# Row maxima from 48-row products in the array's row halves, with stacks loaded for two groups at a time, in a cross-attention and ternary-FFN kernel

## What is computed

```
q = layernorm(x) @ Wq ; k, v = split(ctx @ Wkv)      # 32 heads of 16
q, k = axial_rope(q, pos), axial_rope(k, pos)
w = softmax(q k^T / 4)                               # 4 x 32 heads, 512 x 512 each
x = x + (w v) @ Wout + bout
h = gelu(bitlinear(layernorm(x), w_fc))              # ternary weights, quantised activations
x = x + bitlinear(h, w_proj)
```

## Time and profile before

| | |
|---|---|
| Median of 3 runs | 771.08 us (770.41 to 771.29) |
| Profiled execution | 771.07 us, span in the trace 769.3 us |
| TensorE busy | 754.0 us (98%) |
| VectorE busy | 661.9 us (86%) |
| ScalarE busy | 481.9 us (63%) |
| GpSimd busy | 430.1 us (56%) |
| Chain that ended last | TensorE 87% of the span |
| DMA | 117.24 MB, mean 152 GB/s |
| Granted TensorE clock | 1.00 over nearly all of the span |

### The profile page before, as it was taken

How to read it: one execution, slowest core, us unless ns; L and a number is a source line. 1 busy time by engine, 2 the same in 40 slices (tenths; PEclk the granted TensorE clock), 3 DMA queues, 4 the chain that set the end, 5 groups by cost and what they waited for, 6 DMA issues and landing times.

```text
span 769.3 us, 11882 instructions
## 1 busy us (share of the span) xinstructions
PE 754.0 (98%) x3886; PEld 342.9 (45%) x3886; DVE 661.9 (86%) x927; ACT 481.9 (63%) x830; POOL 430.1 (56%) x501
## 2 busy tenths in 40 slices
PE   5999999999999999999999999999999999999998
PEld 3887877333323322332233223345554455555443
DVE  7888999788888888889888888479998889998895
ACT  4787766787788777788878888765323433333330
POOL 5787776675345446456446557665564845564310
PEclk9999999999999999999999999999999999999999
DMA  8588996555587778887777896326566575544655
GB/s 279 176 219 249 267 260 167 138 141 132 139 170 147 152 157 138 161 179 144 151 162 162 180 192 154 73 69 136 116 135 124 101 147 114 119 96 96 114 106 136
DMA packets 178862, 117.24 MB, mean 152 GB/s; under 512 B 119746, under 2 KB 150514, under 8 KB 178802
## 3 DMA queue, kind: packets, MB, share of 16 engines
q1 hardware_dynamic: 178802, 116.49, 67.6%
HBM read 64.50 MB, written 25.43 MB: 117 GB/s over the span
## 4 chain that ended last, share of the span: by engine, by line
PE 87%; DMA 4%; DVE 2%; ACT 2%; POOL 2%; SPq 1%; issue 1%; POOLq 0%; DVEq 0%; ACTq 0%
PE banks L741 15%; PE banks L725 14%; PE banks L1040 14%; PE banks L1025 14%; PE banks L702 12%; PE banks L297 8%; PE banks L1006 6%; DMA stack_words<-max_rows 2%; PE banks L328 1%; DMA max_rows<-max_parts 1%; PE banks L713 1%; SPq L619 1%; PE banks L280 1%; SPq L257 1%; POOL attn_words L527 0%
## 5 line engine op out<-in xcount | busy, mean ns | idle before, releaser
L815 ACT ACTIVATE probs_words<-banks 128x512 f32<-128x512 f32 x512 | 290.7, 596 | 70.7 <-PE banks L725 57.9
L795 DVE TENSOR_REDUCE maxima<-banks 128x2 f32<-128x1024 f32 x240 | 283.2, 1216 | 41.4 <-PE banks L702 41.4
L725 PE MATMUL banks<-stack_words 98*128 98x512 bf16 x512 | 173.6, 382 | 2.2 <-DMA stack_words<-max_rows 1.2
L702 PE MATMUL banks<-stack_words 96*128 96x512 bf16 x480 | 143.0, 379 | 0.0
L741 PE MATMUL banks<-probs_words,late_words 128*32 128x512 f32 x1024 | 136.4, 605 | 0.0
L725 PEld LDWEIGHTS banks<-stack_words 98*128 98x128 bf16 x512 | 48.7, 96 | 158.0 <-ACT probs_words L815 109.1
L1025 PE MATMUL banks<-ternary_words,late_words 128*128 128x512 f16 x512 | 113.1, 379 | 0.0
L1040 PE MATMUL banks<-ternary_words,stack_words 128*128 128x512 f16 x512 | 112.9, 379 | 0.0
L1224 ACT ACTIVATE probs_words<-probs_words,h_moments 128x2048 f32<-128x2048 f32 (+1 forms) x17 | 32.2, 1901 | 120.6 <-DVE h_moments L1103 120.6
L826 POOL TENSOR_SCALAR neg_max<-maxima 128x16 f32<-128x16 f32 x32 | 8.3, 260 | 145.4 <-DVE maxima L795 145.4
L1025 PEld LDWEIGHTS banks<-ternary_words,late_words 128*128 128x128 f16 x512 | 49.8, 98 | 60.5 <-issue 0.8
(11 more groups left out here) (157 smaller groups left out, 1065.2 us busy)
## 6 DMA issues: line engine op xcount, KB each, us to landing
o_rows<-late_words SPq DMA_DIRECT2D x32, 256.0 KB, 3.4
k_parts<-ternary_words SPq DMA_DIRECT2D x48, 128.0 KB, 3.0
q_parts<-ternary_words SPq DMA_DIRECT2D x48, 128.0 KB, 2.5
stack_words<-q_parts SPq DMA_DIRECT2D x32, 192.0 KB, 3.2
stack_words<-k_parts SPq DMA_DIRECT2D x96, 64.0 KB, 2.7
stack_words<-k_parts SPq DMA_DIRECT2D x32, 192.0 KB, 2.7
attn_words<-in_x_dram SPq DMA_DIRECT2D x16, 256.0 KB, 4.0
probs_words<-in_L_ffn_w_fc_dram SPq DMA_DIRECT2D x16, 256.0 KB, 3.6
```

Source lines behind the costliest of these rows:

```text
L702: mm = self.nc.tensor.matmul(self.score_slot[j % 2][:, i], self.mem.q_stack[0:STACK, slot, head, c * P:(c + 1) * P], self.mem.k_stack[0:ST ...
L725: self.nc.tensor.matmul(self.st_bank[(g * 16 + k) % self.ST_BANKS], self.mem.k_stack[0:STACK + 2, slot, head, c * P:(c + 1) * P], self.mem ...
L795: dve.tensor_reduce(self.maxima[:, g % 2, 2 * j:2 * j + 2], self.score_slot[j % 2], AX.X, ALU.max).then_inc(self.scores_read, 1)
L815: act.activation(self.probs[:, c, head, :], self.st_bank[(g * 16 + k) % self.ST_BANKS], ACT.Exp, scale=1 / math.sqrt(HEAD)).then_inc(self. ...
```

## The change

`scores` and `early_scores` use three of the six part products (48 rows, `MAIN`) in place of six (96). The stacks are laid out so that for heads 0 and 1 the three lie on partitions 0 to 47, for heads 2 and 3 on 64 to 111. A place of `scores` now does head h and head h + 2 of the same chunk: two 48-row products, one on each half of the array's rows, one to each bank of the slot. The turned products run over 114 rows, of which 16 are zero: rows 96 to 111 for the first two heads, 0 to 15 for the others. The zeros come from a strip that GpSimd clears (`row_zeros`, after its third `spread`) and two DMAs (`clear_rows`, SP step 4); begin_late_stacks copies them for a third pair of slots, in `late_words`.

Stacks are loaded for two groups at a time, in two halves of 7 and 8 DMAs with 2 KB rows; a group's first product waits for all 15. Pair 0 is loaded whole at the projection's step 8, pair 1 at steps 12 and 14; in the attention a half follows per step. The scores run two places ahead (`LEAD`). `save_sums` moves behind the third reduction of a step.

```diff
-STACK = 6 * HEAD
+MAIN = 3 * HEAD
+HALF_ROWS = 64
+MAX_ROW = HALF_ROWS + MAIN
+STACK = MAX_ROW + 2
...
-STACK_LOADS = DMA * 7
+STACK_PAIRS = 3
+STACK_LOADS = DMA * (7 + 8)
...
+    def clear_rows(self, sp, rows_set):
+
+        sp.wait_ge(self.row_ones_set, 2)
+        for first, heads in ((STACK - 2 - HEAD, slice(0, 2)), (0, slice(2, 4))):
+            sp.dma_start(self.mem.both_stacks[first:first + HEAD, :, heads].rearrange("p n h c -> p n (h c)").bitcast(F32),
+                         self.row_zeros.unsqueeze(1).to_broadcast([HEAD, 2 * STACK_SLOTS, SEQ])).then_inc(rows_set, DMA)
...
+    def load_stacks(self, sp, pair, half):
+
+        mem, g = self.mem, 2 * pair
+        for i in range(2):
+            sp.wait_ge(self.prj.parts_stored[i], PAIR_STORES * (g // HG + 1))
+        need(sp, self.st_ready, (g - 2 * STACK_PAIRS + 2) * 16)
+        for t, where, runs in ((0, mem.q_parts, self.Q_RUNS[half]), (1, mem.k_parts, self.K_RUNS[half])):
+            src = where[g:g + 2].rearrange("g t (d h) c -> (t d) g (h c)", h=GH)
             for to, part, count in runs:
...
+    def wait_stacks(self, pe, g):
+        pe.wait_ge(self.stacks_loaded[g // 2 % STACK_PAIRS], (g // 2 // STACK_PAIRS + 1) * STACK_LOADS)
+
+    def main_product(self, out, g, head, c):
+
+        first = head // 2 * HALF_ROWS
+        rows = slice(first, first + MAIN)
+        return self.nc.tensor.matmul(out, self.stack(0, g)[rows, head, c * P:(c + 1) * P], self.stack(1, g)[rows, head, :],
+                                     start=True, stop=True)
...
-        for i in range(2):
-            c = j % 2 * 2 + i
-            mm = self.nc.tensor.matmul(self.score_slot[j % 2][:, i],
-                                       self.mem.q_stack[0:STACK, slot, head, c * P:(c + 1) * P],
-                                       self.mem.k_stack[0:STACK, slot, head, :], start=True, stop=True)
+        for half in range(2):
+            mm = self.main_product(self.score_slot[j % 2][:, half], g, j // CHUNKS + 2 * half, j % CHUNKS)
         mm.then_inc(self.scores_ready, 1)
...
-                              self.mem.k_stack[0:STACK + 2, slot, head, c * P:(c + 1) * P],
-                              self.mem.q_stack[0:STACK + 2, slot, head, :], start=True, stop=True
+                              self.stack(1, g)[0:STACK, head, c * P:(c + 1) * P],
+                              self.stack(0, g)[0:STACK, head, :], start=True, stop=True
...
-            if s < GROUPS and not begun:
-                self.scores(pe, s, 2 * c)
+            if not begun:
+                self.scores_ahead(pe, ahead)
...
+        EARLY_LOADS = {8: (0, (0, 1)), 12: (1, (0,)), 14: (1, (1,))}
...
-                    if j == 1 and s >= 3:
+                    if j == 3 and s >= 3:
                         att.save_sums(dve, s - 3)
...
             pool.wait_ge(att.rows_set, DMA)
+            pool.wait_ge(prj.piece_ready[1], 4)
+            pool.memset(prj.row_zeros, 0.0).then_inc(prj.row_ones_set, 1)
```

More of the change, by code:

```diff
@@ new lines, in stack, with begin_late_stacks @@
+    def stack(self, t, g):
+        return self.stack_pair(t, g // 2)[:, g % 2]
+    def begin_late_stacks(self, sp):
+        late = self.late_stacks.rearrange("p t s h c -> p (t s) h c")
+        for first, heads in ((MAX_ROW - HEAD, slice(0, 2)), (0, slice(2, 4))):
+            rows = slice(first, first + HEAD)
+            sp.dma_start(late[rows, :, heads].rearrange("p n h c -> p n (h c)"),
+                         self.mem.k_stack[rows, :, heads].rearrange("p n h c -> p n (h c)")).then_inc(self.rows_set, DMA)
+        rows = slice(MAX_ROW, MAX_ROW + 2)
+        sp.dma_start(self.late_stacks[rows, 1].rearrange("p s h c -> p (s h) c"),
+                     self.mem.k_stack[rows, 0:2].rearrange("p s h c -> p (s h) c")).then_inc(self.rows_set, DMA)
@@ L778, in tensor_step @@
                 self.scores_turned(pe, turned, 4 * c + 3)
-            if s < GROUPS and not begun:
-                self.scores(pe, s, 2 * c + 1)
+            if begun:
+                self.scores_ahead(pe, ahead)
+            self.scores_ahead(pe, ahead + 1)
             if rows_meanwhile and 0 <= turned < GROUPS:
```

82 lines of the change are left out of this document (48 added, 34 removed).

## The result

The changed kernel takes 804.63 us (median of 4 runs, 802.86 to 808.27). The kernel before, run beside it, took 771.18 us. The ratio is 1.0434 (95% interval 1.039 to 1.0478): slower by 33 us, outside the predicted range of 739 to 784 and beyond each of its cases but the one without overlap. The profiled execution took 805.26 us, with a span of 803.5 where it was 769.3 before, so there are 34.2 us to find.

A forecast was written before the change was run, and what follows sets the result against it. The prediction took TensorE, 98% busy, to bound the kernel in projection and attention. Its terms summed to 771.1 - 7 + 7 + 4 + 0.3 = 775.4, given as 775 us, with a range of 739 to 784.

The forecast's parts named there:

- What bounds the kernel: Whole kernel: TensorE, 98% busy, sets the pace in projection and attention, and nothing on it is hidden.
- The scores in the attention: Attention: the two products of a pair overlap, but changes of cut eat most of it; 7 us saved (5 to 12).
- Cheap switches: Rival, attention: a change to row halves costs little or nothing; 744 us (731 to 757), chance 0.36.
- The early scores: Projection: 32 single 48-row products without a partner each pay 0.18 to 0.27 us for switches; 7 us added (4 to 9).
- The first load: Projection: the first early score waits for 15 DMAs instead of 7; 4 us added (3.8 to 5).
- The rest: Remaining edits: GpSimd's memset at the start adds 0.3 us (0 to 0.5); clear_rows, wider turned products and the moved copy nothing.
- the margin that I named against the rival: Attention: a half's last DMA lands 9.2 us after the split; with 0.5 more still under the 9.9 of seven reductions.
- No overlap, 825: Rival, attention: the two products of a pair don't overlap, 43 us more; 825 us, chance 0.04.
- Second half late, 789: Rival, attention: the second half of a stack pair lands late, about 1 us every other step; 789 us, chance 0.07.

The follow-up runs named there:

- experiment 1: The changed kernel with load_weight behind the stack loads and the maxima in every step; 792.72 us, 1.0247.
- experiment 3: The changed kernel with the 32 early scores taken over rows 0 to 111 in place of 48 rows; 795.75 us, 1.0303.
- experiment 4: The changed kernel with pair 0 loaded in halves at projection steps 8 and 10, the first early score waiting for the first half only; 796.56 us, 1.0299.
- experiment 5: The changed kernel with each quarter's second pair of scores right behind weigh_v, five changes of cut instead of six; 800.65 us, 1.035.
- experiment 8: experiment 6 with each quarter's second pair of scores right behind weigh_v, as in experiment 5; 770.30 us, 0.9975.
- experiment 2: The kernel before, with only load_weight moved ahead of the stack loads in odd attention steps; 806.79 us, 1.045.
- the best version: experiment 10 with the two places of lead spread over three quarters of step 2 and second halves' q part issued a step earlier; 766.69 us, 0.9939.
- experiment 6: The changed kernel with the edits of experiment 1, experiment 3 and experiment 4 together; 780.06 us, 1.0079.
- experiment 10: experiment 8 with both halves of pair 2 loaded in attention step 2; 768.54 us, 0.9951.

## Why the prediction was wrong

**What bounds the kernel** was right, and so was the reading that TensorE has no cover in either stage: what experiments 1, 3, 4, 5 and 8 gave back to it showed in the time, in whole or in part.

**The scores in the attention, 7 us saved (bounds 5 and 12).** The mechanism held, and against the rival that I gave 0.36: the halves overlap in full, and the change of cut eats the gain. The Trainium skill, TensorEngine Tiling (Array Packing), Tiling Modes, says that a change of mode drains the array, and the Trainium skill, TensorE: Matmul & The Clock Gate, Part 3, that products in distinct row groups run together; the chain above agrees with both, with 0.10 us more at each change and 0.32 for a pair. The term was mis-sized: I took 0.09 and 0.08 from `weigh_v`, where 0.10 and 0.10 are paid, and put 0.41 for a pair with its switches where 0.32 + 0.32 - 0.22 = 0.42 is measured. At 480 changes that is the difference between 7 us and the 2 that the steps show. I had written that 0.02 moves the sum by 10 us; then 5 was no lower bound.

**The early scores, 7 us added (bounds 4 and 9).** 8.6 by the chain; experiment 3 takes the 0.27 a product away. Right in mechanism, and at 0.27 it is the upper of the two prices I gave for one, so nothing is covered. Two changes of 0.10 leave 0.07 of it; that this is the weights of the f32r product behind is my reading of the earlier trace rows and isn't measured by itself.

**The first load, 4 us added (3.8 to 5).** The place and the mechanism were right, the sizes low. I counted 14 issues at 0.50 and got 64.4 for the last; the profile has 65.24, since the first came 0.9 us later than before (58.33 for 57.39) and the queue stood 0.5 us between the halves, while an issue took 0.47. The step that failed is the one behind it. I took a wait of 4 us to cost 4 us, and left out that TensorE comes back from it at the lower clock level; it cost 1.6 us more, seen in the row of 4.32. In the kernel before that wait was 0.41 us, and the windows of the earlier trace rows are at 1.00, so none of my rows showed the fall; it could have stood as a cost of unknown size.

**The rest.** The memset took 0.52 us (I had 0.3, and 0.5 at the most) and moved nothing: the projection step that began at 31.39 begins at 31.21. clear_rows, the 114 rows and the copy of the sums cost nothing, as written.

**What was not in the sum: 20 us.** This is the step that made the prediction wrong. I walked along the SP queue for the stacks, counted their DMAs and their landing, and priced a late second half at 14 us with a chance of 0.07. I overlooked that `load_weight` had changed places in odd steps, past `load_stacks` and `load_max`. Pricing each moved step with the queue it moves past would have given it: the trace of the kernel before has the operation that it waits for in every step, right behind the split of the earlier trace rows, and experiment 2 shows that this alone is worth 35 us in the kernel before. With it, the margin that I named against the rival (9.2 + 0.5 under 9.9, so 0.2 us) was gone at once, since the queue stands some 3 us at `load_weight`. The rival named the right victim and the wrong cause, its landing of 2.8 us and 0.5 to 1.5 more was short of the 4.76 in the case shown, and its price left out that a wait can drag low-clock time behind it, as much again in that case.

**The rivals.** *Cheap switches, 744*: refuted by the chain (0.32 behind each pair) and by the steps of 11.28 us. *No overlap, 825*: refuted, the two halves are one entry of 0.32 us. *Second half late, 789*: it happened, for the reason above, at 20 us and not 14.

By these terms the sum is 771.1 - 2.1 - 0.5 + 8.6 + 6.7 + 20.7 = 804.5, with the profiled execution at 805.26. The 20.7 are a difference: the attention's 18.1, plus the 2.1 that the pairs gain and 0.5 from a shorter step at the end; experiment 1 took 17.4 of them away. The 0.8 left over lie in the projection. What stays open: what brings the clock down at the start of the attention in some runs and not in others, and what order of the queue would have pair 2 in time; in the best version one step still loses 6 us to it.

## What to carry to other kernels

Two products on row halves save the time of one only where no change of cut is paid for them: place products of one cut next to each other, put row halves right beside column strips where both occur, and count a change of cut as nearly half of a 512-column product (0.10 for 0.22 us). Read a diff of a queue line by line: an instruction that waits for another engine is harmless at the end of its queue's turn, and costs all that is behind it when it is moved to the front, so look for what each moved DMA waits for and who needs the next ones soonest. And look at the granted clock behind a wait on TensorE: slower products may follow that cost as much as the wait, or none may.

## What the runs showed of the hardware

- In this kernel a change between whole rows and row halves, or column strips, costs about 0.10 us each way in a stream of 512-column products (0.32 in place of 0.22 behind it, and one change less per quarter is 2.82 against 2.72 us). Going from column strips directly to row halves is one such change.
- Two products on different row halves, to different banks, start within 5 ns of each other (at 241.60 and 258.20 us) and take 0.32 us with the change ahead of them, as one turned product behind a change does.
- A single row-half product between f32r products costs 0.27 us beyond its stream (8.57 against 7.76 us for three), and none of that over all rows (7.75).
- TensorE came back from some waits near the lower level of its clock, at 0.50 to 0.59: after the 4 us around 66, after 1.57 us at 250, after 3.49 us at 164. In the first two cases the windows 4 us later are at 1.00 and 0.98 again. The Trainium skill, TensorE: Matmul & The Clock Gate, Part 1, describes a clock gate with these two levels, which falls when the array has been idle; these three agree. I had not expected that a wait within a full stream would bring it and double what the wait costs.
- The length of a wait doesn't tell the fall by itself. In the projection of experiments 4, 6 and 10 the clock stayed at 1.00 behind waits of 0.62, 1.59 and 1.86 us. At the start of the attention it was 0.50 in experiment 6 behind waits of 0.49 us at most, and 1.00 in the changed kernel behind the same ones. No run here shows what decides.
